# Cross-attention and FP4 feed-forward on one core: six residual sums by ScalarE and Pool, the last two x groups' absolute values in PSUM, the last group normalised by ScalarE

## What is computed

```python
def fp4_quant_dequant(x):               # blocks of 16 along the last axis
    scale = max(|xb|) / 6, at least 1e-12
    q = nearest of {0, .5, 1, 1.5, 2, 3, 4, 6} to |xb| / scale, with sign, times scale

gate = fp4_linear(x, w_gate)            # 128 -> 352
y    = fp4_linear(x, w_up)              # 128 -> 352
h    = silu(gate) * y
out  = fp4_linear(h, w_down)            # 352 -> 128

x = x + xattn(ctx, layernorm(x), mask)
x = x + ffn(layernorm(x))
```

## Time and profile before

| | |
|---|---|
| time, median of 3 runs | 218.21 us (218.11 to 219.34) |
| profiled execution: its time, its span | 219.57 us, 217.6 us |
| mean granted TensorE clock | 0.973 of full |
| TensorE busy | 187.8 us (86%) |
| VectorE busy | 176.5 us (81%) |
| Pool busy | 139.3 us (64%) |
| ScalarE busy | 131.8 us (61%) |
| instructions | 5689 |

### The profile page before, as it was taken

The page is one execution under the profiler, slowest core; times in us unless marked ns, Lnnn a source line. Parts: engine busy times, 40 slices in busy tenths (PEclk is TensorE's granted clock), DMA queues, the critical chain, the costliest instruction groups (busy, mean ns, idle before and its releaser), DMA issues.

```text
span 217.6 us, 5689 instructions
## 1 busy us (share of the span) xinstructions
PE 187.8 (86%) x2045; PEld 141.5 (65%) x2045; DVE 176.5 (81%) x391; ACT 131.8 (61%) x264; POOL 139.3 (64%) x203
## 2 busy tenths in 40 slices
PE   0839988979998999998998998796898988899963
PEld 0318574856967769587696775475676766677753
DVE  6417785898799876978769987999999999999941
ACT  2362697957878877798786744364455383665441
POOL 6272737188969592672926577676689875777750
PEclk9985999999999999999999999699999999999998
DMA  6999632040200000000000000000101010101111
GB/s 190 268 293 345 225 115 81 7 144 3 96 3 5 3 0 0 5 3 3 0 3 5 0 5 0 0 0 2 50 3 48 0 48 3 48 2 51 48 49 48
DMA packets 13665, 11.97 MB, mean 55 GB/s; under 512 B 766, under 2 KB 10558, under 8 KB 13630
## 3 DMA queue, kind: packets, MB, share of 16 engines
q1 hardware_dynamic: 13078, 11.29, 16.8%
q10 hardware_dynamic: 560, 0.33, 0.5%
HBM read 9.52 MB, written 2.10 MB: 53 GB/s over the span
## 4 chain that ended last, share of the span: by engine, by line
PE 31%; POOL 20%; issue 14%; DVE 7%; ACT 4%; POOLq 0%; DVEq 0%; ACTq 0%
POOL hq L372 7%; POOL wq_y L357 5%; PE bank L890 4%; PE bank L946 4%; PE bank L949 3%; PE bank L899 3%; PE bank L900 2%; PE bank L878 2%; PE bank L970 2%; POOL xn L254 2%; ACT xn L411 2%; PE a_pair L841 2%; POOL sch L364 2%; PE bank L841 2%; ACT val L423 2%
## 5 line engine op out<-in xcount | busy, mean ns | idle before, releaser
L970 PE MATMUL bank<-wdT,hT 128*128 128x128 f32 x192 | 27.1, 278 | 4.1 <-issue 3.3
L946 PE MATMUL bank<-guT,xqT 128*128 128x352 f32 x64 | 25.5, 481 | 4.3 <-DVE hh L732 4.3
L372 POOL TENSOR_TENSOR hq<-wq_u,sch 128x704 f32<-128x704 f32 x16 | 22.6, 1410 | 9.5 <-DVE wq_u L759 9.4
L970 PEld LDWEIGHTS bank<-wdT,hT 128*128 128x128 f32 x192 | 23.9, 191 | 5.4 <-issue 4.4
L949 PE MATMUL bank<-guT,xqT 128*128 128x352 f32 x64 | 25.0, 473 | 0.0
L357 POOL TENSOR_TENSOR wq_y<-hh,ivh 128x704 f32<-128x704 f32 x16 | 22.5, 1407 | 3.9 <-DVE ivh L747 3.3
L878 PE MATMUL bank<-cT,wsT 128*128 128x512 f32 x32 | 16.9, 655 | 6.5 <-DMA cT<-in_ctxT 6.5
L477 ACT ACTIVATE mask_bc<-bank 128x352 f32<-128x352 f32 x32 | 14.7, 458 | 12.3 <-PE bank L946 12.3
L545 ACT COPY hT<-bank 128x384 f32<-128x384 f32 x32 | 15.2, 476 | 10.2 <-PE bank L958 10.2
L532 ACT ACTIVATE a_pair<-wq_y 128x704 f32<-128x704 f32 x16 | 12.2, 763 | 14.8 <-DVE wq_u L759 14.4
L612 DVE TENSOR_REDUCE den<-prob 128x8 f32<-128x512 f32 x32 | 19.8, 666 | 0.0
(11 more groups left out here) (117 smaller groups left out, 497.2 us busy)
## 6 DMA issues: line engine op xcount, KB each, us to landing
cT<-in_ctxT SPq DMA_DIRECT2D x8, 512.0 KB, 5.2
x_all<-in_x SPq DMA_DIRECT2D x8, 256.0 KB, 5.5
mask_bc<-in_mask_rows SPq DMA_DIRECT2D x8, 256.0 KB, 6.3
out_y<-mask_bc SPq DMA_DIRECT2D x8, 256.0 KB, 2.2
wsT<-in_WsT ACTq DMA_DIRECT2D x1, 256.0 KB, 4.2
w_all<-in_wg SPq DMA_DIRECT2D x1, 176.0 KB
w_all<-in_wu SPq DMA_DIRECT2D x1, 176.0 KB
w_all<-in_wd SPq DMA_DIRECT2D x1, 176.0 KB
```

Source lines behind the costliest of these rows:

```text
L372: nc.gpsimd.tensor_tensor(hq[i][:, :, 0:I].rearrange("p t (n k) -> p t n k", k=BLK), rh[i][:, :, :].rearrange("p (t n) k -> p t n k", t=2) ...
L946: nc.tensor.matmul(gu_bank[2 * n % 3][:, 0:I], xqT[g % 2][:, t], guT[:, 0, :], start=True, stop=True).then_inc(pe_g, 1)
L970: last = nc.tensor.matmul(d_bank[:, j * P:(j + 1) * P], hT[n % 2][:, c, :], wdT[:, c, :], start=(c == 0), stop=(c == 2))
```

## The change

Four things change, all in the feed-forward loops.

1. The residual of groups 0 to 5 (`D_BY_ACT = 6`) is no longer one VectorE instruction. ScalarE copies d_bank into y_out at the start of its step 4g+12 (`down_evac`), and Pool adds x to it there after y_unit of unit 2g+5 (`residual_sum`). The next down matmul into d_bank waits for ScalarE's copy. Each group's sum has a semaphore of its own. Groups 6 and 7 stay as they were.
2. The absolute values of x groups 6 and 7 go into the first bank of `a_pair` (`a_last`), where `ah` of the h units also lies. So ScalarE's absolute of group 6 waits until unit 2 has been rounded, that of group 7 until unit 8, and `h_abs` of units 3 and 9 waits until the x group has been rounded. `s3_round` of both groups stands directly behind the product of step 9 and of step 21.
3. Group 7 is normalised by ScalarE (`normalise2`, step 14, four instructions) with a bias that Pool works out (`bias2_of`); Pool's `xn2_of` of it is gone.
4. Group 7's block maxima, reciprocal and absolute value stand one step later, and its `xq_of` on Pool one unit later (u = 11 for 10).

```diff
+D_BY_ACT = 6
...
+        a_last = a_pair[:, 0, :].rearrange("p (n k) -> p n k", k=BLK)
...
             def store(g):
-                sp.wait_ge(yo_ok, g + 1)
+                sp.wait_ge(yo_ok[g], 1)
...
+            def residual_sum(g):
+                pool.wait_ge(d_ok, g + 1)
+                ys = y_out[g % 2][:, :, :]
+                nc.gpsimd.tensor_tensor(ys, ys, x_all[:, tiles(g), :], ALU.add).then_inc(yo_ok[g], 1)
+
+            def bias2_of(g):
+                pool.wait_ge(rstd2, g + 1)
+                pool.wait_ge(nm2_ok, g + 1)
+                nc.gpsimd.tensor_tensor(nb2[:, tiles(g)], nm2[:, tiles(g)], rs2[:, tiles(g)], ALU.mult).then_inc(nb2_ok, 1)
...
-                if u == 6:
-                    xn2_of(NG - 1)
+                if u == 5:
+                    bias2_of(NG - 1)
...
-                if u == 10:
+                if u == 11:
                     xq_of(NG - 1)
+                if u % 2 and 0 <= (u - 5) // 2 < D_BY_ACT:
+                    residual_sum((u - 5) // 2)
...
             def y2_abs(g):
                 act.wait_ge(y2_ok, g + 1)
                 past(act, r2_ok, g)
-                nc.scalar.activation(a2[:, :, :], y2[:, :, :], ACT.Abs, scale=MAGIC).then_inc(a2_ok, 1)
+                if g >= NG - 2:
+                    act.wait_ge(rh_ok, 3 if g == NG - 2 else 9)
+                nc.scalar.activation(a2[:, :, :] if g < NG - 2 else a_last, y2[:, :, :], ACT.Abs,
+                                     scale=MAGIC).then_inc(a2_ok, 1)
...
             def h_abs(u):
                 act.wait_ge(yh_ok, u + 1)
                 past(act, rh_ok, u)
+                if u in (3, 9):
+                    act.wait_ge(r2_ok, NG - 1 if u == 3 else NG)
...
+            def down_evac(g):
+                act.wait_ge(pe_dn, (g + 1) * TILES)
+                past(act, out_d[g % 2], 16 * (g // 2))
+                nc.scalar.copy(y_out[g % 2][:, :, :].rearrange("p t d -> p (t d)"), d_bank[:, :]).then_inc(d_ok, 1)
+
+            def normalise2(g):
...
+                for j in range(TILES):
+                    n = g * TILES + j
+                    last = nc.scalar.activation(xn2[:, j * NB_X:(j + 1) * NB_X, :].rearrange("p n k -> p (n k)"),
+                                                x_all[:, n, :], ACT.Identity, bias=nb2[:, n:n + 1], scale=rs2[:, n:n + 1])
+                last.then_inc(xn2_ok, 1)
+
             for m in range(NT + LAG + 1):
+                if (m - LAG - 1) % TILES == 0 and 0 <= (m - LAG - 1) // TILES - 1 < D_BY_ACT:
+                    down_evac((m - LAG - 1) // TILES - 1)
...
-                if m == 19:
+                if m == 14:
+                    normalise2(NG - 1)
+                if m == 20:
                     y2_abs(NG - 1)
...
                 if m < NT:
                     h_product(m)
-                if m < NT and (m - LAG) % TILES == 0 and on((m - LAG) // TILES - 1):
-                    residual((m - LAG) // TILES - 1)
+                if m in (9, 21):
+                    s3_round(NG - 2 if m == 9 else NG - 1)
...
-                if m == 9:
-                    s3_round(NG - 2)
                 if m == 11:
                     stats2(NG - 1)
-                if m == 15:
+                if m == 16:
                     block_max(NG - 1)
-                if m == 17:
+                if m == 18:
                     block_reciprocal(NG - 1)
-                if m == 20:
-                    s3_round(NG - 1)
...
                 if j == 0:
-                    past(pe, yo_ok, g)
+                    past(pe, d_ok, min(g, D_BY_ACT))
+                    if g > D_BY_ACT:
+                        pe.wait_ge(yo_ok[g - 1], 1)
```

More of the change, by code:

```diff
@@ L88, in xattn_ffn @@
         st2, mv2 = sb("st2", [P, NT, 6]), sb("mv2", [P, NT, 2])
-        nm2, ve2, rs2 = (sb(n, [P, NT]) for n in ("nm2", "ve2", "rs2"))
+        nm2, ve2, rs2, nb2 = (sb(n, [P, NT]) for n in ("nm2", "ve2", "rs2", "nb2"))
         cT = [sb(f"cT{s}", [P, 2, GT]) for s in range(4)]
@@ L160, in xattn_ffn @@
             sem(n) for n in ("pe_x0", "x0_ok", "pe_t", "t_ok", "pe_g", "pe_u", "pe_dn"))
-        sg_ok, h_ok, amh_ok, uph_ok, ivh_ok, sch_ok, yh_ok, ah_ok, uh_ok, rh_ok, hq_ok, yo_ok = (
+        sg_ok, h_ok, amh_ok, uph_ok, ivh_ok, sch_ok, yh_ok, ah_ok, uh_ok, rh_ok, hq_ok, d_ok = (
             sem(n) for n in ("sg_ok", "h_ok", "amh_ok", "uph_ok", "ivh_ok", "sch_ok", "yh_ok", "ah_ok",
-                             "uh_ok", "rh_ok", "hq_ok", "yo_ok"))
+                             "uh_ok", "rh_ok", "hq_ok", "d_ok"))
+        nb2_ok = sem("nb2_ok")
+        yo_ok = [sem(f"yo_ok{g}") for g in range(NG)]
         x_tiles = x.rearrange("(n p) d -> p n d", p=P)
@@ L644, in s3_round @@
             def s3_round(g):
+                a = a2[:, :, :] if g < NG - 2 else a_last
                 dve.wait_ge(a2_ok, g + 1)
                 dve.wait_ge(y2_ok, g + 1)
-                nc.vector.scalar_tensor_tensor(out=u2[:, :, :], in0=a2[:, :, :], scalar=FLOOR * MAGIC, in1=y2[:, :, :],
+                nc.vector.scalar_tensor_tensor(out=u2[:, :, :], in0=a, scalar=FLOOR * MAGIC, in1=y2[:, :, :],
                                                op0=ALU.max, op1=ALU.add).then_inc(u2_ok, 1)
@@ L650, in s3_round @@
                 past(dve, xq_ok, g)
-                nc.vector.scalar_tensor_tensor(out=r2[:, :, :], in0=a2[:, :, :], scalar=FLOOR * MAGIC, in1=u2[:, :, :],
+                nc.vector.scalar_tensor_tensor(out=r2[:, :, :], in0=a, scalar=FLOOR * MAGIC, in1=u2[:, :, :],
                                                op0=ALU.max, op1=ALU.subtract).then_inc(r2_ok, 1)
@@ L766, in residual @@
                 nc.vector.tensor_tensor(y_out[g % 2][:, :, :], d_bank[:, :].rearrange("p (t d) -> p t d", t=TILES),
-                                        x_all[:, tiles(g), :], ALU.add).then_inc(yo_ok, 1)
+                                        x_all[:, tiles(g), :], ALU.add).then_inc(yo_ok[g], 1)
             for m in range(NT + LAG + 2):
@@ L788, in _ @@
                     block_reciprocal(NG - 2)
-                if m == 9:
-                    s3_round(NG - 2)
                 if m == 11:
                     stats2(NG - 1)
-                if m == 15:
+                if m == 16:
                     block_max(NG - 1)
-                if m == 17:
+                if m == 18:
                     block_reciprocal(NG - 1)
-                if m == 20:
-                    s3_round(NG - 1)
-                if m >= NT and (m - LAG) % TILES == 0 and on((m - LAG) // TILES - 1):
+                if (m - LAG) % TILES == 0 and D_BY_ACT <= (m - LAG) // TILES - 1 < NG:
                     residual((m - LAG) // TILES - 1)
```

5 lines of the change are left out of this document (added).

## The result

The changed kernel takes 222.27 us (median of 4 runs, 221.16 to 223.4) against 218.5 for the kernel before in the same comparison (4 runs, 218.11 to 219.34). The ratio is 1.0157, 95% interval 1.0109 to 1.0205: slower, by 3.8 us; whether the loss is over 2% the interval leaves open. The forecast was 220.9 in 216.5 to 222.9. One execution of the kernel before (313.96 us, mean granted clock 0.581) and a few that lay over 1.5% above the fastest of their kernel are left out of every ratio, though not out of the medians and ranges given.

A forecast was written before the change was run, and what follows sets the result against it. VectorE and TensorE were both taken as nearly full, TensorE setting the pace late. Terms of 0.0 up to product 24, then +1.4, +0.1, +0.2 and +1.0, made +2.7 on the 218.21 median: 220.9 us, range 216.5 to 222.9.

The forecast's parts named there:

- the likeliest one: The forecast's own case, waits plus a fallen TensorE clock: 219.8 to 222.8 us, chance 0.40.
- The hold: Steps 8 and 20: ScalarE's absolute waits for a rounding, +1.5 each; cheaper rounding pairs leave net +0.4 and +0.3 us.
- Residuals on VectorE: Steps 11 to 23: four residuals taken off VectorE at 0.48 each, -1.9 us.
- Pool: Up to product 24: VectorE's small L744 waits behind a Pool filled by the sums, net +1.0 us, bounds 0 and 2.5.
- The last x group: Step 25: TensorE waits for the later x multiplication, product 26 +1.4 us; then TensorE's pace for five tiles, +0.1.
- Tail: Unit 14's hq behind the sixth sum on Pool, with the sixth residual's relief: together +0.2 us.
- The clock: After the first hold: idle TensorE drops to the 1.2 GHz level, +1.0 us, bounds 0 and 2.9.
- the waits, without the clock: Rival: all terms but the clock's apply, +1.7, 219.9 us; chance 0.27.
- The freed time survives: Rival: no L744 waits, last x group in time, only TensorE's stream as floor: -4.1, 214.1 us; chance 0.15.
- Relief and waits cancel: Rival: Pool's waits near nothing and clock holds, 218.9 us, or a cheaper rounding pair, 218 us; chance 0.18.
- PSUM frees nothing: Rival: rounding pairs each cost 1.1 more, 223.1 us with the rest; counted inside the range, no separate chance.

The follow-up runs named there:

- e6: The kernel before with only the absolute values of x groups 6 and 7 in PSUM, taken behind silu and hT copy of the next step: 216.78 us.
- e1: The changed kernel with Pool's x multiplication of group 7 (`xq_of`) back behind unit 10: 221.22 us.
- e8: The changed kernel with Pool's six residual sums cut to 32 of 512 columns: 222.18 us.
- e10: The changed kernel with residuals back on VectorE, absolute values taken late as in e6 and the x multiplication placed as in e1: 217.79 us.
- e11: e10 with group 7's block maxima and reciprocal back in steps 15 and 17: 217.07 us.
- e7: The changed kernel with absolute values taken late as in e6 and the x multiplication placed as in e1: 218.6 us.
- e12: e7 with group 7's block maxima and reciprocal back in steps 15 and 17: 217.91 us.
- e3: The changed kernel with 16 extra TensorE matmuls, whose result nobody reads, in step 9: 220.52 us.
- e2: The changed kernel with the absolute values of x groups 6 and 7 back in SBUF, without the shared bank's waits: 220.28 us.

## Why the prediction was right, point by point

The time, 222.27, lies in the range, 1.4 above the forecast, and the case was the likeliest one. The sum was +2.7; the stretches behind product 8 give +4.1. What was seen in advance was the mechanism, part by part; that the total came so near owes something to the clock, whose price varies from execution to execution. By its terms:

1. **The hold: right.** Counted from product 8, TensorE's transposition was due 3.3 behind it (148.3 less 145.01) and came at 3.46; product 9 was due at +3.66 and came at +3.70. Pair 0.68 and 0.69 as taken, though the first pair, with Pool idle beside it, would not have shown whether PSUM helps; the second and e6's do. In e1, where the clock does not interfere, 9 to 10 takes 3.24, 1.14 less than before, as worked out. The second pair, with the silu behind the h absolute, cost 0.48 against the 0.3 and 0.2 of the sum.
2. **Residuals on VectorE: right in size.** 22 to 24 is 0.47 shorter; 0.48 was taken. But here the x multiplication has left Pool's unit 10 too: with it back in its place (e1) L787 waits 0.2 for Pool, and the stretch is only 0.26 shorter than before.
3. **Pool: the net about right, two terms mis-sized.** The sum is 1.28 long, not 1.06; the range of 0.9 to 1.4 held it. The estimate by the Trainium skill (GPSIMD Engine Reference, section 3.1), 1.33, was nearer than the row I chose: a two-input add takes Pool 1.88 times the 0.68 of L766, where its broadcast multiplication of the same size takes 1.06. The L787 waits over 0.19 from product 8 to 24 are 0.53, 1.06 and 0.64 against 0.47 and 0.45 before: +1.3, where +1.0 stood. The 0.53, at 155.98, comes with the fallen clock: without a fall (e1) L787 takes 0.19 there, the waits are 0.62, 0.47 and 0.63, and the term is +0.8. So 0.5 of the +1.3 is also in item 6. Unit 6 was named and is the long one. (From product 12 to 20 the waits make +1.25 and two residuals -0.96, where +0.50 is measured; 0.2 are in neither.) But the cause that I gave, that a full Pool is met in a sum, is too simple: shrunk to 0.25 in e8, the sums leave waits of 1.13 to 1.19, all behind hq. And part 4's move of the block steps, which the prediction costed at nothing, is worth 1.3 us by itself where no sums stand (e10, e11); it hides in the change only since the sums have moved L787 onto Pool's instructions already (e7, e12).
4. **The last x group: right.** 24 to 26 is 1.42 longer (1.4 taken); e1 takes 1.0 of it away. What is left there, 0.42, is one more L787 wait (0.62 at 190.29, behind an hq that stands behind the fourth sum). From there five tiles take 10.91, 0.08 over before (0.1 taken).
5. **Tail: mis-sized.** +0.53, not +0.2. The sum takes 1.24 from start to start, not 1.02, and these 0.22 go into it in full, as hq 14 starts right behind it.
6. **The clock: the mechanism right, the size too small.** It fell in the idle stretch where it was foretold, and was low for 6.8 us, 5.2 of them with TensorE at work. It cost 2.1 us in the profile, the 0.53 of L787 included, where 1.0 was taken (bounds 0 and 2.9). In the medians e3 puts it at 1.75. This is the largest part of the 1.4 by which the forecast was low. In e8 it cost 0.4 and in e1 nothing, so the 1.0 is a fair middle, and a single size for it was never to be had.

Of the rivals, "the waits, without the clock" is what single executions of e1 show (9 to 12 in 8.51), so it was a real alternative from run to run. "The freed time survives" needed product 31 before 200.4; it came at 205.09. "Relief and waits cancel" is close to what e7 does (218.6), once the two orders are mended. "PSUM frees nothing" is refuted by the 0.68 and 0.69 from 181.69 on, beside a busy Pool, where e2 has 1.76 and 1.76.

What stays open: where the clock is full throughout, the kernel before still has runs near 216.5 and runs near 218.5; the one traced execution of it (219.57, mean clock 0.973) is neither, and doesn't show what parts them.
